# Masked cross attention: value waves issued in pairs, and the additive mask written by ScalarE for three score blocks in eight

## What is computed

```python
v = einsum('nlhd,ed->nlhe', values.reshape(n, 8192, 16, 32), Wv)   # and k, q likewise
energy = einsum('nqhd,nkhd->nhqk', q, k)                            # 512 x 8192 for each of 16 heads
energy = where(mask == 0, -1e+20, energy)
attention = softmax(energy / sqrt(512.), axis=3)
out = einsum('nhql,nlhd->nqhd', attention, v).reshape(n, 512, 512)
return out @ Wo.T + bo
```

## Time and profile before

| | us |
|---|---|
| median of 3 runs | 4477.82 (4474.61 to 4483.54) |
| the profiled execution | 4484.0 |
| span in its trace | 4481.9 |
| of it, layer 0's score loop, first to last ScalarE mask write | 484.0 to 1481.0 |

### The profile page before, as it was taken

The page is one execution under the profiler, slowest core; times in us unless marked ns, Lnnn a source line. Parts: engine busy times, 40 slices in busy tenths (PEclk is TensorE's granted clock), DMA queues, the critical chain, the costliest instruction groups (busy, mean ns, idle before and its releaser), DMA issues. The chain is left out here.

```text
span 4481.9 us, 50984 instructions
## 1 busy us (share of the span) xinstructions
PE 3975.0 (89%) x17680; PEld 2213.4 (49%) x17680; DVE 2993.9 (67%) x3608; ACT 2351.9 (52%) x3611; POOL 1667.8 (37%) x984
## 2 busy tenths in 40 slices
PE   7995899999999686678999779999999988769997
PEld 6883344444443341147777434444444335447775
DVE  4333878777785359936777567777778644467776
ACT  2221577777777333313676426666666631337674
POOL 0001487778878425400000036666566630000000
PEclk9997899999999779889999869999999988789998
DMA  8998566666666200022888546666666540318886
GB/s 310 328 336 273 150 153 152 155 154 148 156 149 144 80 14 0 0 85 113 302 301 302 203 132 154 152 154 152 140 151 144 120 99 26 79 59 305 304 300 227
DMA packets 301550, 751.69 MB, mean 168 GB/s; under 512 B 55793, under 2 KB 89329, under 8 KB 268016
## 3 DMA queue, kind: packets, MB, share of 16 engines
q1 hardware_dynamic: 245136, 560.20, 37.1%
q0 software_dynamic: 47456, 171.46, 19.0%
q10 hardware_dynamic: 8704, 16.78, 1.1%
HBM read 484.23 MB, written 98.37 MB: 130 GB/s over the span
## 5 line engine op out<-in xcount | busy, mean ns | idle before, releaser
L749 ACT ACTIVATE prob<-psum 128x512 f32<-128x512 f32 x1552 | 891.7, 595 | 430.7 <-PE psum L647 393.7
L647 PE MATMUL psum<-q_stack,k_ring 98*128 98x512 f32 x2048 | 1006.1, 510 | 19.8 <-ACT prob L749 14.4
L924 POOL TENSOR_TENSOR den_pool<-den_pool,prob 128x1024 f32<-128x1024 f32 x372 | 937.2, 2519 | 220.2 <-DVE den_pool L836 184.7
L622 PE MATMUL psum<-k_ring,q_stack 96*128 96x512 f32 x2048 | 691.7, 422 | 106.3 <-DVE row_max L807 36.1
L803 DVE TENSOR_REDUCE row_max<-psum 128x1 f32<-128x1024 f32 x512 | 615.3, 1220 | 238.0 <-PE psum L622 235.0
L807 DVE CUSTOM_DVE_ANT_0 psum<-psum,mask_q 128x1024 f32<-128x1024 f32 x512 | 627.3, 1233 | 206.5 <-PE psum L622 191.2
L647 PEld LDWEIGHTS psum<-q_stack,k_ring 98*128 98x128 f32 x2048 | 395.2, 194 | 620.7 <-ACT prob L749 274.7
L1891 DVE TENSOR_TENSOR weight_lo<-weight_raw,weight_hi 128x2048 fp32r<-128x2048 f32 x240 | 546.9, 2289 | 163.2 <-ACT weight_hi L1834 162.9
L665 PE MATMUL psum<-prob,x 128*32 128x512 f32 x3104 | 515.7, 610 | 0.9 <-ACT prob L749 0.9
L622 PEld LDWEIGHTS psum<-k_ring,q_stack 96*128 96x128 f32 x2048 | 394.1, 200 | 213.7 <-issue 84.2
L1834 ACT ACTIVATE weight_hi<-weight_raw 128x2048 fp32r<-128x2048 f32 x240 | 454.4, 1916 | 43.2 <-DMA weight_raw<-in_L_ffn_w 25.3
(11 more groups left out here) (422 smaller groups left out, 6385.6 us busy)
## 6 DMA issues: line engine op xcount, KB each, us to landing
weight_raw<-in_L_ffn_w SPq DMA_DIRECT2D x120, 1024.0 KB, 6.7
den_dma<-prob POOLq DMA_DIRECT2D x204, 512.0 KB, 4.9
k_ring<-k_hi SPq DMA_DIRECT2D x1024, 64.0 KB, 2.2
weight_raw<-in_L_ffn_Wu SPq DMA_DIRECT2D x60, 1024.0 KB, 7.2
weight_raw<-in_L_ffn_Wd SPq DMA_DIRECT2D x60, 1024.0 KB, 4.9
den_dma<-xnT POOLq DMA_DIRECT2D x68, 512.0 KB, 4.9
k_ring<-k_lo SPq DMA_DIRECT2D x512, 64.0 KB, 2.4
ctxT<-in_ctxT SPq DMA_DIRECT2D x16, 1024.0 KB, 9.5
```

The costliest lines, as they stand in the source:

```text
L622: ins = e.matmul(max_banks(q)[:, a * KC:(a + 1) * KC], q_stack[h % n_q][0:QROWS, i * P:(i + 1) * P], k_ring[0:QROWS, (n + a) % kring, :], ...
L647: e.matmul(k.bank(b % 2), k_ring[:, n % kring, kt * P:(kt + 1) * P], q_stack[h % n_q][:], start=not masked, stop=True, skip_group_check=ma ...
L749: e.activation(prob[b // 2 % n_p][:, b % 2, :], k.bank(b % 2), ACT.Exp, scale=scale).then_inc(s_exp, 1)
L924: e.tensor_tensor(den[:], den[:], tile, ALU.add).then_inc(s_dpool, 1)
```

## The change

The number of waves that are issued together is a parameter now: two in the masked attention (layer 0), one in the other. `step` gives both waves of a pair the pair behind which the later one may start, so they stand behind every fourth pair, between a block with b % 8 == 1 and one with b % 8 == 2. ScalarE writes the mask for the blocks with b % 8 in (2, 3, 6), where it did for 2 and 6; the mask matmuls of layer 0 go from 768 to 640, and ScalarE's mask writes from 256 to 384. For the odd block 3 the write stands behind `exponentials(2g + 1)`.

```diff
+MASK_FIRST = (2, 3, 6)
...
-    def __init__(self, by_pe):
-        self.values, self.sums = [], []
+    def __init__(self, by_pe, together):
+        self.values, self.sums, self.together = [], [], together
...
     def step(self, w):
 
-        return -(-(self.values[w][-1] + 1) // 2)
+        last = min(w - w % self.together + self.together, self.count) - 1
+        return -(-(self.values[last][-1] + 1) // 2)
...
-    waves = Waves(sums.by_pe)
+    waves = Waves(sums.by_pe, 2 if masked else 1)
...
-                if masked and b % 4 == 2:
-                    e.wait_ge(s_pre, b // 4 + 1)
+                mask_there = masked and b % 8 in MASK_FIRST
+                if mask_there:
+                    e.wait_ge(s_pre, len(MASK_FIRST) * (b // 8) + MASK_FIRST.index(b % 8) + 1)
                 elif b >= 2:
                     e.wait_ge(s_exp, b - 1)
-                if masked and b % 4 != 2:
+                if masked and not mask_there:
                     e.matmul(k.bank(b % 2), k.ident_big[:], masks[1][:, t, :], start=True, stop=False)
                 e.matmul(k.bank(b % 2), k_ring[:, n % kring, kt * P:(kt + 1) * P], q_stack[h % n_q][:],
-                         start=not masked, stop=True, skip_group_check=masked and b % 4 == 2).then_inc(s_score, 1)
+                         start=not masked, stop=True, skip_group_check=mask_there).then_inc(s_score, 1)
...
                 exponentials(2 * g)
-                if masked and g % 2 == 0:
+                if masked and (2 * g + 2) % 8 in MASK_FIRST:
                     mask_first(2 * g + 2)
...
                 exponentials(2 * g + 1)
+                if masked and (2 * g + 3) % 8 in MASK_FIRST:
+                    mask_first(2 * g + 3)
```

## The result

The changed kernel takes 4517.98 us (median of 4 runs, 4513.4 to 4522.9) against 4478.65 us before. The ratio is 1.0086, with a 95% interval of 1.0071 to 1.0102: slower by 39 us, where 35 us were forecast.

A forecast was written before the change was run, and what follows sets the result against it. TensorE's own stream was taken as the bound, with ScalarE's chain close behind. Rounds +33 us and once-a-head work +1 to +2 gave +35 on the median 4477.8: 4513 us, range 4482 to 4530 (8 in 10).

The forecast's parts named there:

- The chain of 1.90 us: Layer 0's score loop: from a score to the score taking ScalarE's mask in the same bank, never under 1.90 us.
- The 1.19 us to a mask matmul: Layer 0's score loop: from an unmasked score to the mask matmul two blocks on, never under 1.19 us.
- The round: Eight blocks of layer 0's score loop, double wave to double wave: from 7.50 to 7.76 us, +33 us in all.
- The saved passages: Paired waves save one passage into and out of the 32-column form: 0.31 us per eight blocks, open weight load included.
- Rival C: Two waves in a row save nothing, the second starting 0.99 behind the first: 14 us on top, 4527; chance 0.10.
- The open weight load: Before score(6), block 6 of eight: the load idles until ScalarE's mask write, 0.34 instead of 0.23 us.
- Once a head: Per-head work in layer 0: head_out gives back 0.34 a head, m_hi_rows costs 0.43, take_values 0.16; together +1 to +2 us.
- The clock: Layer 0's score loop: the granted clock should stay at 1.00.
- my +2 us for the work once a head: Follow-up forecast for paired waves with ScalarE's masks for blocks 2 and 3: +2 us once a head, kernel about 4461.
- Rival A: TensorE's stream alone decides: eight blocks take 6.96 us, gain 69 us, 4409; chance 0.10, shared with anything towards no difference.
- both waits: TensorE's stalls on ScalarE per eight blocks: 0.15 us before mask(4), 0.54 us before score(6).
- the 0.15 before mask(4): Block 4's mask matmul needs block 2's exponential: at 3.06 instead of 2.91 us behind the double wave, stall 0.15.

The follow-up runs named there:

- the version with four masks: Kernel before, single waves kept, with ScalarE writing the masks for blocks 2, 3, 6 and 7 of eight: 4478.16 us, ratio 0.9999.

## Why the prediction was right, point by point

- **The bound and the chain.** Right. The chain of 1.90 us from score to score over exponential and mask write, read at the only place in the trace before where no wave covered it, is 1.90 in the changed kernel. The 1.19 us to a mask matmul holds too (902.30 to 903.50 is 1.20).
- **The round.** Forecast 7.76, measured 7.76. The saved passages are 0.03 or so off in their parts: the second wave starts 0.90 behind the first (0.88 forecast), and score(2) 1.85 behind the double wave (1.87). Rival C, in which two waves in a row save nothing, is out.
- **The open weight load.** Right: score(6) is 0.34 from the next matmul (905.44 to 905.78), so the load was not pulled ahead across the wait.
- **Once a head.** The round of head_out was 0.23 shorter than before (0.08 forecast, +0.26 less 0.34), the last round of a head 0.58 longer (0.54 forecast), the first 0.43 (0.42). Sum +2.10 us a head, 2.18 by my steps.
- **What I missed.** The last head. It has no maxima matmuls left to fill the stream, so TensorE runs into ScalarE sooner: 6.8 us longer than before, where I had counted it like the others with 2.1. With these 4.7 us, and 2.8 that heads 4, 8 and 12 took less over the others than before (4.1 in sum against 6.9), the forecast of +35 becomes +37; the loop grew by 36.4. The second of these is the draw of one execution each, so that the two partly cancel is luck. Four rounds of this head show the longer wait alone, 7.36 to 7.38 us against 6.50 to 6.52; the first, 8.47 against 7.20, also has the stretch at a granted clock of 0.50. The timeline of TensorE in the last head of the changed kernel, score(4), score(5) and score(6):

```profile
1496.75 0.59 PE L652 MATMUL psum<-q_stack,k_ring 98*128 98x512 f32 x1
...
1497.24 0.59 PE L652 MATMUL psum<-q_stack,k_ring 98*128 98x512 f32 x1
1498.66 0.50 PE L652 MATMUL psum<-q_stack,k_ring 98*128 98x512 f32 x1 [0.83 <-ACT psum L759]
```

  The chain is the same, 1.91 us from score(4) to score(6), but score(5) comes sooner: TensorE stands 0.83 us here, against 0.39 in the middle of the loop.
- **The clock.** "Should stay at 1.00" is right for the mean of the loop and for the quiet rounds, not for the 3.4 us from 1460.4. The same holds for what was said of the kernel before, with its 3.4 us from 1034.0.
- **Once a head, for other versions.** For pairs with masks 2 and 3 my +2 us for the work once a head was wrong: the rounds with head_out and m_hi_rows took 0.3 us each more than the quiet ones had led me to expect, some 9 us a kernel. ScalarE's extra rows stand in these rounds, so I take them to go at its pace already; the move of head_out fits that, but no run measured it by itself.
- **Rival A** needed both waits gone. With a mask matmul at block 6 the large one was, and the round was 7.32 us, not the 7.19 that rival A gives for that version: the 0.15 before mask(4) stayed. Of rival A's 69 us against the kernel before, nothing measurable was there to have in that version, and with the products moved in both, 8 us of loop and 6 of median.

## What to carry to other kernels

Before an instruction that separates a producer's trigger from its consumer is moved or bunched, look at what hides behind it: the longest chain over the other engine, read where nothing covers it (a loop's first round is a good place), against the stream time that will be left between the two ends. A wait on the other engine's result that costs nothing in the profile may be free only because of an unrelated instruction in front of it. And where a round shrinks as reckoned but the kernel does not, compare the rounds one by one: the gain may be lost in a few rounds that another pair of engines decides. Before such a loss is put down to the version, look at a trace of unchanged code, to see how much these rounds vary by themselves.

## What the runs showed of the hardware

A VectorE product of two 128x128 scratch operands took 0.28 us alone and up to 3.15 us beside GpSimd's additions (3.31 in the version with four masks), and each that waited ended 0.15 or 0.16 us behind an addition's end, while reciprocals of the same size, with one operand, took 0.93 to 0.95 us. On GpSimd itself the product took 0.45 to 1.04 us. Moving 24 of them won 13 us. ScalarE's copy of 8-bit data into the accumulator bank took 0.60 us for 512 columns and 0.39 for 256. Its next instruction starts 0.49 us behind a 0.60 us exponential, and 0.63 if it waits for that exponential's end.
